# A Mamba-2 mixer with squares, weight scaling and the state's decay products on GpSimd, and the first convolution tap ahead of its step

## The reference

```python
def _mamba2_layer(h, Wi, cw, cb, dtb, Alog, Dh, gw, Wo):
    zxbcdt = h @ Wi                       # h is RMS-normalised before
    z, xBC, dt = split(zxbcdt)            # 256 | 512 | 8
    conv = cb + sum(xp[:, k:k + L, :] * cw[:, k] for k in range(4))
    xBC = silu(conv)
    ...
    def step(hs, inp):                    # state [8 heads, 32, 128]
        hs = hs * dA_t + dtx_t * B_t
        y = einsum('bhpn,bn->bhp', hs, C_t)
    y = ys + Dh * xs                      # the skip
    y = _rmsnorm(y * silu(z), gw)
    return y @ Wo
for l in range(4): h = h + _mamba2_layer(_rmsnorm(h, w[l]), ...)
```

## Time and profile before

| what | value |
|---|---|
| median of 3 runs | 1162.11 us (1161.69 to 1162.46) |
| profiled execution, its own time | 1162.99 us |
| its span | 1161.0 us |
| busy in the span: PE, DVE, ACT, POOL | 86%, 84%, 76%, 58% |
| TensorE's granted clock in the steps | full (the page's row has 9 in tenths there) |
| mixer steps (first S[1] to last) | 72.4 to 791.9 us |

### The profile page before, as it was taken

How to read it: one execution, slowest core, us unless ns; L and a number is a source line. 1 busy time by engine, 2 the same in 40 slices (tenths; PEclk the granted TensorE clock), 3 DMA queues, 4 the chain that set the end, 5 groups by cost and what they waited for, 6 DMA issues and landing times.

```text
span 1161.0 us, 25184 instructions
## 1 busy us (share of the span) xinstructions
PE 993.7 (86%) x6136; PEld 559.7 (48%) x6136; DVE 977.1 (84%) x1801; ACT 884.2 (76%) x1724; POOL 676.3 (58%) x853
## 2 busy tenths in 40 slices
PE   5799999999899999999999999985788767999980
PEld 4244544445444444454445444542444445777760
DVE  6779999999999999999999998974778775888865
ACT  5688999999899999999999999984556534655640
POOL 0267577766776677656655765672244551666661
PEclk9789999999999999999999999998888888999995
DMA  5111242224222432210001000100000115676638
GB/s 141 34 34 33 89 156 86 88 87 153 91 86 87 142 102 86 78 32 22 22 23 31 22 22 23 27 7 1 19 28 28 37 33 180 223 232 226 223 116 217
DMA packets 85584, 97.84 MB, mean 84 GB/s; under 512 B 20698, under 2 KB 65888, under 8 KB 85536
## 3 DMA queue, kind: packets, MB, share of 16 engines
q1 hardware_dynamic: 80544, 88.83, 24.2%
q0 software_dynamic: 4992, 8.48, 2.2%
HBM read 59.67 MB, written 37.83 MB: 84 GB/s over the span
## 4 chain that ended last, share of the span: by engine, by line
PE 35%; DVE 26%; issue 18%; ACT 6%; POOL 3%; DVEq 2%; DMA 1%; ACTq 0%; SPq 0%; POOLq 0%
DVE cv L1354 9%; PE bank L494 4%; PE bank L562 4%; PE bank L681 2%; PE bank L667 2%; DVE M L1370 2%; PE bank L683 2%; PE bank L682 2%; DVE cv L1350 2%; PE bank L619 2%; PE bank L693 2%; PE bank L695 2%; PE bank L692 2%; PE bank L658 2%; PE bank L640 2%
## 5 line engine op out<-in xcount | busy, mean ns | idle before, releaser
L1354 DVE SCALAR_TENSOR_TENSOR cv<-bank,PAR,cv 128x511 f32<-128x511 f32 (+2 forms) x384 | 274.1, 742 | 15.7 <-ACT cv L963 2.8
L1370 DVE SCALAR_TENSOR_TENSOR M<-E,bank 128x512 f32<-128x512 f32 x256 | 168.3, 678 | 20.7 <-ACT E L951 11.4
L1679 POOL TENSOR_TENSOR yt<-yt,ti 128x384 f32<-128x384 f32 x64 | 64.0, 1000 | 203.6 <-DVE ti L1470 203.6
L494 PE MATMUL bank<-hn,WA 128*128 128x512 f32 x256 | 144.9, 649 | 41.0 <-DVE cv L1354 40.6
L951 ACT ACTIVATE E<-bank 128x512 f32<-128x512 f32 x256 | 149.0, 595 | 31.9 <-DVE M L1370 30.1
L1710 POOL DMA_INDIRECT RS<-y,XR x92 | 98.8, 1074 | 78.7 <-DVE y L1567 55.4
L1703 POOL DMA_INDIRECT XS<-stage,IDX x64 | 65.9, 1029 | 79.2 <-DVE run L1329 62.1
L1101 ACT ACTIVATE hr<-bank,W1B 128x512 f32<-128x512 f32 x92 | 63.4, 689 | 56.7 <-PE bank L683 49.8
L562 PE MATMUL bank<-M,dtx 128*32 128x128 f32 x2048 | 82.9, 279 | 15.6 <-DVE o_sb L1389 15.1
L494 PEld LDWEIGHTS bank<-hn,WA 128*128 128x128 f32 x256 | 40.6, 194 | 111.9 <-issue 74.0
L1497 DVE TENSOR_TENSOR hL<-hr,hH 128x512 fp32r<-128x512 f32 x124 | 87.1, 702 | 4.3
(11 more groups left out here) (245 smaller groups left out, 2633.8 us busy)
## 6 DMA issues: line engine op xcount, KB each, us to landing
XS<-PADT SPq DMA_DIRECT2D x32, 520.0 KB, 4.3
WA<-w_in SPq DMA_DIRECT2D x192, 64.0 KB, 1.8
W1B<-WD SPq DMA_DIRECT2D x23, 514.0 KB
W2B<-WD SPq DMA_DIRECT2D x23, 512.5 KB
WD<-WS SPq DMA_DIRECT2D x16, 512.0 KB, 2.7
XR<-XS SPq DMA_DIRECT2D x23, 260.0 KB
RW<-w_in SPq DMA_DIRECT2D x18, 256.0 KB, 4.4
WO_raw<-w_out SPq DMA_DIRECT2D x32, 128.0 KB, 3.6
```

What stands on the lines that cost most here:

```text
L494: mm(bank[t % 2][:, :], WA[t][:, :], hn[:, :], start=True, stop=True).then_inc(pj_mm, 1)
L1354: stt(out=cv[t][:, s:L], in0=src[:, 0:L - s], scalar=PAR[:, bass.ds(cw + 3 - s, 1)], in1=cv[t][:, s:L], op0=ALU.mult, op1=ALU.add).then_in ...
L1370: stt(out=M[i % 4][:, :].rearrange("p (n t) -> p n t", n=4), in0=E[i % 2][:, :].rearrange("p (n t) -> p n t", n=4), scalar=1.0, in1=bank[5 ...
```

## The change

Nothing is computed otherwise. Work moves between engines and inside their orders:

- ScalarE's `norm_square` goes: `WDT` and `sqh` are made on GpSimd (`step_weights`, `square_h`), the square one step earlier. Its two `WO` copies go there too (`output_weights`).
- ScalarE's `norm_log` stood between `decay_exp(6)` and `decay_exp(7)`, and now stands after `decay_exp(7)`.
- VectorE's two decay products into `stmp` go to GpSimd. Between them VectorE makes the skip sums (`with_skip`).
- VectorE's `tap(0, 0)` of step k + 1 stands before the `ti` products of the body k. The taps of tiles 0 and 1 stand in another order, and `causal_products` is ahead of three of them.
- On GpSimd all of it stands behind `own` and ahead of the `yt`, `y2` work.

```diff
@@ ScalarE, body
                 if N:
-                    norm_square(k + 1)
...
                 if B:
                     row_exp(1)
-
-                    wait(act, s_wo, 16 * (j + 1))
-                    wait(act, out_mm, j)
-                    gw = act.snap(j // NB * NPAR + C_GW)
-                    for t in range(2):
-                        f(WO[:, t * DM:(t + 1) * DM], WO_raw[:, t * DM:(t + 1) * DM], ACT.Copy,
-                          scale=PAR[:, bass.ds(gw + t, 1)]).then_inc(wos_a, 1)
                     decay_exp(6)
+                if B:
+                    decay_exp(7)
                 if N:
                     norm_log(k + 1)
-                if B:
-                    decay_exp(7)
-                if N:
                     norm_root(k + 1)
@@ VectorE, body
                 if A:
-                    tap(0, 0)
-                    tap(0, 1)
-                    tap(0, 2)
-                    tap(1, 1)
-                    tap(0, 3)
-                    tap(1, 2)
+                    tap(k, pk, 1, 1)
+                    tap(k, pk, 0, 1)
                 if B:
                     causal_products()
+                if A:
+                    tap(k, pk, 0, 2)
+                    tap(k, pk, 0, 3)
+                    tap(k, pk, 1, 2)
+                if B:
                     apply_decay(0)
...
                     cp(S[1][:, :], bank[4][:, 0:DI]).then_inc(s_v, 1)
-                    wait(dve, dec_a, j + 1)
                     for c in range(2, NC):
-                        wait(dve, s_v, 5 * j + 2 * c - 3)
-                        tt(stmp[:, :].rearrange("p (h d) -> p h d", h=NH), S[c - 1][:, :].rearrange("p (h d) -> p h d", h=NH),
-                           dec[:, (c - 1) * NH:c * NH].unsqueeze(2).to_broadcast([P, NH, HD]), ALU.mult).then_inc(s_v, 1)
-                        wait(dve, s_v, 5 * j + 2 * c - 2)
+                        with_skip(c - 2)
+                        wait(dve, decay_p, 2 * j + c - 1)
...
+                    if N:
+                        tap(k + 1, dve.snap((k + 1) // NB * NPAR), 0, 0)
@@ GpSimd, body, behind own_rows(0) and own_rows(1)
+                if N:
+                    step_weights(k + 1)
+                if B:
+                    output_weights(j)
+                if N:
+                    square_h(k + 2)
+                if B:
+                    wait(pool, dec_a, j + 1)
+                    for c in range(2, NC):
+                        wait(pool, s_v, 3 * j + c - 1)
+                        tt(stmp[:, :].rearrange("p (h d) -> p h d", h=NH), S[c - 1][:, :].rearrange("p (h d) -> p h d", h=NH),
+                           dec[:, (c - 1) * NH:c * NH].unsqueeze(2).to_broadcast([P, NH, HD]), ALU.mult).then_inc(decay_p, 1)
                     for t in range(2):
                         wait(pool, fin_v, 4 * j + 3 + t)
```

More of the change, by code:

```diff
@@ L866, in _ @@
             modulate_input(0, 0)
-            norm_square(0)
+            f(WDT[:, :], PAR[:, C_WDT:C_WDT + 32], ACT.Copy).then_inc(wdt_done, 1)
+            act.wait_ge(hup, 1)
+            f(sqh[:, :], h[:, 0:L], ACT.Square).then_inc(sqh_done, 1)
             for b in range(1, 4):
@@ L1028, in body @@
                     f(ecs[:, :], cum[:, :], ACT.Exp, scale=-1.0, bias=cum[:, CH - 1:CH]).then_inc(dta_a, 1)
-                if N:
-                    norm_square(k + 1)
-                elif A:
+                if A and not N:
                     square_h(0)
@@ L1335, in gate, with tap @@
                 dve.wait_ge(setup_v, 1)
+            def tap(k, first, t, s):
+                cw = first + C_CW + 4 * t
+                src = bank[t % 2]
+                if s == 0:
+                    wait(dve, pj_mm, 6 * k + t + 1)
+                    wait(dve, silu_a, 6 * (k - 1) + SILU_TURN[t] + 1)
+                    ts(cv[t][:, :], src[:, :], PAR[:, bass.ds(cw + 3, 1)], PAR[:, bass.ds(first + C_CB + t, 1)],
+                       ALU.mult, ALU.add).then_inc(tap_v[t], 1)
+                else:
+                    wait(dve, tap_v[t], 4 * k + s)
+                    stt(out=cv[t][:, s:L], in0=src[:, 0:L - s], scalar=PAR[:, bass.ds(cw + 3 - s, 1)],
+                        in1=cv[t][:, s:L], op0=ALU.mult, op1=ALU.add).then_inc(tap_v[t], 1)
             def body(k, odd, A, B, C, N):
@@ L1413, in body @@
                 if A:
-                    tap(2, 1)
+                    tap(k, pk, 2, 1)
                 if B:
@@ L1417, in body @@
                 if A:
-                    tap(2, 2)
+                    tap(k, pk, 2, 2)
                 if C:
@@ L1433, in body @@
                 if A:
-                    tap(3, 3)
+                    tap(k, pk, 3, 3)
                 if B:
@@ L1442, in body, with with_skip @@
                     add_mamba(0)
+                if N and not B:
+                    tap(k + 1, dve.snap((k + 1) // NB * NPAR), 0, 0)
                 if B:
+                    def with_skip(t):
+                        wait(dve, y_mm, 4 * j + 4)
+                        wait(dve, fin_p, 4 * j - 2 + 2 * t)
+                        stt(out=yt[t][:, :], in0=conv_rows(t, odd + 1), scalar=PAR[:, bass.ds(pj + C_D + t, 1)],
+                            in1=bank[6 + t][:, :], op0=ALU.mult, op1=ALU.add).then_inc(fin_v, 1)
                     wait(dve, st_mm, 2 * j + 1)
@@ L1460, in body @@
                         halve(0)
-                    for t in range(2):
-                        if t == 0:
-                            wait(dve, y_mm, 4 * j + 4)
-                        wait(dve, fin_p, 4 * j - 2 + 2 * t)
-                        stt(out=yt[t][:, :], in0=conv_rows(t, odd + 1), scalar=PAR[:, bass.ds(pj + C_D + t, 1)],
-                            in1=bank[6 + t][:, :], op0=ALU.mult, op1=ALU.add).then_inc(fin_v, 1)
+                    if N:
+                        tap(k + 1, dve.snap((k + 1) // NB * NPAR), 0, 0)
                     for t in range(2):
@@ L1579, in expert @@
                         low_slots(i + 1)
+            tap(0, 0, 0, 0)
             steps(dve, body)
@@ L1615, in _, with square_h, step_weights, output_weights @@
                            channel_multiplier=0).then_inc(padt_p, 1)
+            def square_h(n):
+                hb = h[:, bass.ds(n % NB * L, L)]
+                wait(pool, hup, n + 1)
+                wait(pool, ms_mm, n)
+                tt(sqh[:, :], hb, hb, ALU.mult).then_inc(sqh_done, 1)
+            def step_weights(n):
+                wait(pool, dt_mm, n)
+                tt(WDT[:, :], PAR[:, bass.ds(pool.snap(n // NB * NPAR + C_WDT), 32)], ones_row[:, 0:32], ALU.mult).then_inc(wdt_done, 1)
+            def output_weights(n):
+                gw = pool.snap(n // NB * NPAR + C_GW)
+                wait(pool, s_wo, 16 * (n + 1))
+                wait(pool, out_mm, n)
+                for t in range(2):
+                    tt(WO[:, t * DM:(t + 1) * DM], WO_raw[:, t * DM:(t + 1) * DM], PAR[:, bass.ds(gw + t, 1)].to_broadcast([P, DM]),
+                       ALU.mult).then_inc(wos_p, 1)
             def body(k, odd, A, B, C, N, W=None):
```

59 lines of the change are left out of this document (21 added, 38 removed).

## The result

| kernel | median us | lowest to highest | ratio to before |
|---|---|---|---|
| before | 1161.9 | 1161.49 to 1162.46 | 1 |
| after | 1195.09 | 1194.24 to 1195.75 | 1.0285 [1.0267, 1.0303] |

The account below looks back on a forecast made before the run. The order of waits in a loop through TensorE and VectorE was taken as the bound. A step becomes 10.99 + 13.50 = 24.49 us against 23.21, +1.28; over 30 steps +38 us, so 1200 us, range 1171 to 1214.

Parts of the forecast that it names:

- O to T: From the end of o_sb to the end of the second ti; forecast to grow from 11.83 us to 13.50.
- T to O: From the end of the second ti to the next o_sb's end; forecast to fall from 11.63 us to 10.99.
- Point 3: ScalarE's log behind decay_exp(7), which waits for apply_decay(5): TensorE's turns start 0.92 us later.
- Point 4: S[2] and S[3] between skip sums, with GpSimd's products: S[3] comes later for L658, 0.75 us a step.
- Point 5: From the second ti to the next o_sb's end: earlier taps let project(2) and project(3) start sooner, 0.64 us less.
- Point 2: ScalarE's copies and square leave where it waits anyway: gain counted as 0, no exponential earlier.
- Point 6: GpSimd's added work, 3.5 us, fits its 5.20 us idle in front of yt; cost 0, also for hn.
- Rival C: GpSimd in the way: hn loses up to 0.8 us a step to the square, 1224 us, half 1212; chance 0.09.
- A: Rival: VectorE is the bound, so each step loses 1.2 us, 1126 us; chance 0.12.
- B: Rival: only one of the two delays, log or chain of S, is real, 1173 or 1178 us; chance 0.15.
- D: Rival: no effect, the 0.64 us gain at the taps and the losses cancel, 1162 us; chance 0.04.

## Why the prediction was right

**The sum.** Without the split, two delays and one gain make up the whole. For the log and the chain the sizes are those measured alone on before, for the taps and GpSimd's work those inside after:

| part | O to T | T to O |
|---|---|---|
| log behind the last exponential | +0.68 | 0 |
| decay products on GpSimd, skip sums between | +0.96 | 0 |
| taps | 0 | -0.62 |
| GpSimd's weights and square | 0 | 0 |
| sum | +1.64 | -0.62 |
| measured, after less before | +1.64 | -0.67 |

The taps' zero is the run with the old taps (13.42 against 13.43). GpSimd's is shown for the square (13.43 with and without), not for its weights. Measured alone on before, the taps cost 0.44 in O to T and GpSimd's work 0.06, so the four parts alone would sum to +2.14: the parts don't add independently, the chain's wait hides the early tap. The 0.05 us that is missing in T to O is before's even body, 11.09 there and 11.00 in the kernels with the log or the chain alone.

**Point 3, the log: mechanism right, somewhat too large.** Forecast 0.92, measured 0.68 to 0.89. The turns' weight load comes 0.69 later relative to O without the split (679.63 - 674.10 = 5.53, before 4.84 from the earlier trace rows) and 1.21 later with it (437.56 - 431.51 = 6.05). The forecast's 5.76 lies between them. The difference is spend's length. The step of the earlier trace rows has the split, and there spend took 0.49 us; without the split it takes 0.23, in the step above 0.75. Each excess over 0.23 shifts every M behind it, and from M the last exponential and the log: 5.76 - 0.26 = 5.50, and 5.50 + 0.52 = 6.02. In before the 0.26 cost next to nothing (O to T 11.83 against 11.79), since the log did not wait for that M there. So one step was read as if it were all steps.

**Point 4, the chain of S: mechanism right, too small.** Forecast 0.75, measured 0.96 alone and 0.97 undone. In the step shown, chunk 3's sums end at 440.66 and L658 starts 2.55 later; before it was 1.74. That is 0.81, and L658 itself takes 1.60 instead of 1.50. The forecast had L658 at its old length, and 0.06 less in front of it. It had also named the right releaser of S[3], GpSimd's second product. S[1], behind a long hn, ended at 440.62 in that step, still before chunk 3's sums.

O to T was thus forecast at 13.50 and is 13.43 and 13.89. The errors of points 3 and 4, 0.24 too much and 0.21 too little, cancel in the steps without the split; that is luck.

**Point 5, T to O: right in size, taken from too high a start.** In the step above, project(2) starts at 449.49, T + 4.07 (forecast 4.20), and project(3) at 452.50 without a wait. The mean is 10.69, forecast 10.99. What was missed is the other body: 11.63 was read in the odd body, the even one already had 11.09. Against the true mean of 11.36 the forecast gave only 0.37, and 0.67 came. This is the larger error of the sum: 0.3 us a step, 9 us too many. The steps with the split went the other way (13.89 against 13.50), 0.39 us in 18 of them, 7 us too few. That the time came out within 5 us of the forecast is in part luck, too.

**Point 2, ScalarE: right.** Its busy time fell by 16 us, and that moved nothing: with only this work gone from ScalarE to GpSimd, the kernel was 10 us slower. In after it waits for M 78 times instead of 38.

**Point 6, GpSimd: cost right, one reason incomplete.** Its additions fit in front of yt, whose wait fell from 5.20 us to 2.12 in the step shown, and from 203.6 to 68.7 us over the span. The square takes 1.04 us, not 1.27, WO 0.43 and WDT 0.26. Rival C's mechanism did occur: hn takes 1.22 us in the mean and up to 1.67, where the running sum's +0.28 had been taken for it. But it cost nothing, since the slack behind it was larger than the 0.48 counted: with hn 0.91 too long, VectorE still waited 0.31 for chunk 3's sums. The run with the square moved shows it: hn back at 0.75, the step unchanged. Where the slack is smaller, VectorE's longer instructions beside GpSimd seem to cost something (argued from differences, not isolated): the steps with the split are 0.29 us longer than those without in before, and 0.58 with GpSimd's work added; 0.50 with the log late, and 0.76 and 1.18 in the two kernels with the chain back on VectorE, which have both.

**The rivals.** A fell: VectorE lost work and gained waits. B fell: each delay shows alone, and both show together. C had the mechanism but not the price. D fell.

The signs that were named came: S[1] to S[1] 24.31 for the 24.5, ScalarE's gap before the last exponential (0.66 for M), the skip sum released by L562, L658 released by S[3], o_sb waiting for L511 in every step instead of 4 times. One sign named for being wrong came too: hn longer than 0.75 us.

## What to carry to other kernels

A move off a busy engine gains nothing by itself when the loop is held by the order of waits; price the hand-over at each joint. Here two products of 0.42 us became two of 0.62 on another engine, with a skip sum in front of each add: 0.96 us a step more on the path, while the 0.92 us taken off VectorE gave nothing back. An instruction that is moved ahead is free only while the engine would wait there, so the same edit of the taps gains some 0.6 us a step beside one edit and next to nothing beside another: cost parts together as well as alone. And read the two or four kinds of step (odd and even, with and without side work) before one of them stands for the average.

## What the runs showed of the hardware

**A small VectorE instruction can be held until GpSimd's instruction ends.** spend (128x32, fp32 to bf16) takes 0.23 us where GpSimd stands still. Of before, GpSimd and VectorE at two places:

```profile
394.28 1.28 POOL L1671 TENSOR_TENSOR h<-h,o_sb 128x512 f32 x1
...
394.61 0.98 DVE L1383 TENSOR_SCALAR spend<-CST,p 128x32 bf16<-128x32 f32 x1
...
417.15 1.27 POOL L1667 TENSOR_TENSOR WS<-RW,WS 128x512 fp32r<-128x512 f32 x1
...
417.97 0.49 DVE L1383 TENSOR_SCALAR spend<-CST,p 128x32 bf16<-128x32 f32 x1
```

It ends at 395.59 and 418.46, 0.03 to 0.04 us behind GpSimd's instruction each time (395.56, 418.42). So it is in all 19 of the 32 steps of before in which spend is longer than 0.24 us; in the 13 others no GpSimd instruction runs beside it. With the split moved, all 32 are short:

```profile
L1382 DVE TENSOR_SCALAR spend<-CST,p x32: 230/232/234, 42.5 to 756.1; 128x32 bf16<-128x32 f32 x32
```

That is where the 0.29 us of a step with the split come from: O to T falls to 11.79 when spend is short, and VectorE's order was not touched. (The edit also lets GpSimd's update of h start earlier, and no run takes that apart. But the rows of before show spend's path: behind it stand an M and the last tap, `tap(3, 3)`, which ends at 396.85 and releases TensorE's project(5), 4.50 us behind O, where it is 3.90 in the steps without the split.)

```profile
396.11 0.74 DVE L1354 SCALAR_TENSOR_TENSOR cv<-bank,PAR,cv 128x509 f32<-128x509 f32 x1
...
396.99 1.10 PE L494 MATMUL bank<-hn,WA 128*128 128x512 f32 x2 [0.43 <-DVE cv L1354]
```

The Trainium skill (SBUF — State Buffer, "Who interferes with whom") says that VectorE's second pair of ports is shared with GpSimd and locked for one of them at a time. These rows agree in that one waits for the other's end; which ports are in use, they don't show. hn agrees too: in after's timeline it starts at 438.63 beside WO's scaling and ends at 440.29, 0.54 us behind the end of the square.

**GpSimd's product of a tensor with itself is shorter than one of two tensors.** The square takes 1.04 us in the median of 32 (128x512 fp32), `y<-yt,zs` of the same shape 1.27 in the earlier trace rows.
